# Four layers in one kernel: one arena for the head buffers, the bias of v folded away, normalisation on four engines, an order by a table of times

## What is computed

```python
h = layer_norm(x, g1, beta1)
q, k, v = h @ w_qkv + b_qkv                     # per window and head
attn = q * scale @ k.T + rel_h(q) + rel_w(q)    # bias by relative position
x = x + softmax(attn) @ v @ w_proj + b_proj
x = x + gelu(layer_norm(x, g2, beta2) @ w1 + b1) @ w2 + b2
```

## Time and profile before

| | before |
|---|---|
| runs, median (lowest, highest) | 798.07 us (797.04, 798.78) |
| profiled execution, its own time | 794.48 us |
| its span | 792.7 us |
| mean granted clock of TensorE | 0.825 |
| instructions | 13858 |

### The profile page before, as it was taken

One profiled execution on the slowest core, in us unless ns is written; L12 is line 12 of the kernel. 1 busy time (PEld: TensorE's weight loads), 2 busy tenths in 40 slices (PEclk: granted clock), 3 DMA queues, 4 the chain that ended last, 5 costly groups with the idle time before them and its releaser, 6 DMA issues.

```text
span 792.7 us, 13858 instructions
## 1 busy us (share of the span) xinstructions
PE 601.9 (76%) x5444; PEld 434.8 (55%) x5444; DVE 314.9 (40%) x846; ACT 224.7 (28%) x420; POOL 125.1 (16%) x154
## 2 busy tenths in 40 slices
PE   7737487797906988878989887387949667997677
PEld 4525365666605645645755655265726454785366
DVE  4325546526212521515242363535344652352203
ACT  2113231263400235213124433003523226222231
POOL 2120202000400231132032230010011210010001
PEclk8666756698856999979989997678986779997799
DMA  5582122130033122344022130612251302100000
GB/s 159 135 197 58 39 59 57 24 72 21 14 86 114 31 80 74 104 121 132 15 75 72 47 104 2 170 27 49 47 145 41 77 19 58 39 2 20 1 0 21
DMA packets 31913, 51.73 MB, mean 65 GB/s; under 512 B 8383, under 2 KB 12719, under 8 KB 31754
## 3 DMA queue, kind: packets, MB, share of 16 engines
q1 hardware_dynamic: 31850, 50.85, 24.8%
HBM read 10.09 MB, written 0.79 MB: 14 GB/s over the span
## 4 chain that ended last, share of the span: by engine, by line
PE 59%; DVE 16%; SPq 8%; DMA 7%; issue 5%; ACT 5%; DVEq 0%; POOL 0%; ACTq 0%
PE PS L1122 56%; DVE NM L1043 3%; DMA QA<-NR 3%; DMA COL<-in_col 2%; DVE STAT L954 2%; PE PS L1140 1%; DMA QA<-KC 1%; SPq L615 1%; PE PS L1214 1%; DVE XN L973 1%; DVE QHL L1016 1%; ACT HT L896 1%; SPq L654 1%; SPq L648 1%; DVE RSTD L965 1%
## 5 line engine op out<-in xcount | busy, mean ns | idle before, releaser
L872 ACT ACTIVATE PT<-PS 98x392 f32<-98x392 f32 (+2 forms) x192 | 96.2, 513 | 319.1 <-PE PS L1122 318.6
L1043 DVE TENSOR_REDUCE NM<-PS 98x2 fp32r<-98x392 f32 (+2 forms) x192 | 108.1, 572 | 146.4 <-PE PS L1122 145.0
L1122 PE MATMUL PS<-QA,KA 128*98 128x196 f32 (+2 forms) x528 | 124.8, 348 | 28.3 <-DMA QA<-NR 20.3
L1122 PE MATMUL PS<-KA,QA 127*98 127x196 f32 (+3 forms) x432 | 105.5, 344 | 48.5 <-issue 33.9
L1122 PEld LDWEIGHTS PS<-QA,KA 128*98 128x98 f32 (+2 forms) x528 | 89.9, 212 | 58.5 <-issue 24.7
L1122 PEld LDWEIGHTS PS<-KA,QA 127*98 127x98 f32 (+3 forms) x432 | 72.8, 217 | 69.8 <-issue 50.2
L1122 PE MATMUL PS<-XT,W 96*128 96x512 f32 x144 | 69.9, 620 | 1.3 <-ACT XT L817 1.3
L1122 PE MATMUL PS<-XT,WQKV 96*96 96x512 f32 x128 | 64.7, 635 | 1.3 <-ACT XT L817 1.3
L1214 PE MATMUL PS<-IDN,NM 120*6 120x120 f32 (+1 forms) x72 | 22.9, 318 | 54.4 <-DVE NM L1043 54.4
L1122 PE MATMUL PS<-PT,V 128*32 128x196 f32 (+2 forms) x672 | 60.6, 407 | 0.9 <-ACT PT L872 0.9
L1122 PE MATMUL PS<-W,HT 128*128 128x192 f32 x288 | 52.6, 343 | 10.9 <-ACT HT L896 10.9
(11 more groups left out here) (91 smaller groups left out, 663.2 us busy)
## 6 DMA issues: line engine op xcount, KB each, us to landing
QA<-QHL SPq DMA_DIRECT2D x72, 96.0 KB, 2.4
KA<-KHL SPq DMA_DIRECT2D x48, 141.0 KB, 2.6
QA<-REL SPq DMA_DIRECT2D x48, 128.0 KB, 2.4
QA<-QHL SPq DMA_DIRECT2D x24, 192.0 KB, 2.7
KA<-KHL SPq DMA_DIRECT2D x24, 192.0 KB, 2.7
W<-in_w SPq DMA_DIRECT2D x6, 576.0 KB, 6.5
QA<-REL SPq DMA_DIRECT2D x48, 64.0 KB, 2.2
KA<-KC SPq DMA_DIRECT2D x12, 235.0 KB
```

The costliest lines, as they stand in the source:

```text
L872: nc.scalar.activation(dst, src, ACT.Exp).then_inc(probs_done.sem, 1)
L1043: nc.vector.tensor_reduce(dst, src, AX.X, ALU.max, negate=True).then_inc(max_done.sem, 1)
L1122: return nc.tensor.matmul(dst, lhsT, rhs, start=start, stop=stop, skip_group_check=loose)
```

## The change

- **Arena.** The four head buffers become one memory ARENA of 5 slots of the wide layer; slots of both kinds are counted from its end. The wide layer's ring grows from 4 to 5. `place_of` gives a head its slot, turned so that the first heads of a new layer lie over the slots that the old one leaves first; `constants` becomes one step per slot that waits only for the last old head lying there. In padded layers two slots get their constants by one pair of DMAs, and q and k of a head go in one DMA (QKHL14 holds both), which waits for both splits.
- **v.** Its bias is no longer added. `fold` multiplies the bias by WP and adds the result to the row of WP that holds the bias of proj. v of padded layers is copied by ScalarE, that of the wide layer by VectorE. The buffers BV with padded values shrink to a constant.
- **Normalisation.** `ln` keeps the statistics on VectorE; `rs` computes the reciprocal root in sixteen operations on GpSimd; `xn` scales on ScalarE; `turn` is on TensorE as before.
- **k** of padded layers is permuted by ScalarE when it is copied out of PSUM. PT16 holds 4 heads; the clearing of PT14 is gone. gelu runs in four quarters. `norm` is two steps.
- **Spectral layer.** Both halves come at the end, in memory of their own (LATE, over the arena); s1 runs per image.
- **Loads.** The columns and relative tables of layers 1 and 2 and the second half of x are issued at the head of `weights` of phase 0.
- **Order.** `ordered` sorts the steps by a table, TIMES, with one time per step in units of heads from the phase's first scores.

```diff
-        self.ring = 6 if self.pads else 4
+        self.ring = 6 if self.pads else 5
+        self.turn = 2 if self.pads else 3
+        self.slot_room = self.tiles * (HT_ + self.keys)
+        self.const_dmas = 2 if self.pads else 3
         self.rel_row = 3 * head_dim if self.pads else head_dim
         self.mask_row = self.rel_row + (64 if self.pads else 32)
-        self.aug_dmas = 3 if self.pads else 6
+        self.aug_dmas = 2 if self.pads else 6
...
+def place_of(p, h):
+    return (HEADS * (p % 2) + h + L.turn) % L.ring
+
+def slot_start(L, s):
+
+    return L16_ROOM - (L.ring - s) * L.slot_room
+
+L16_ROOM = LAYERS[1].ring * LAYERS[1].slot_room
+
+def last_over(p, s):
+
+    L, before = PHASES[p].L, PHASES[p - 1].L
+    first, end = slot_start(L, s), slot_start(L, s) + L.slot_room
+    over = [h for h in range(HEADS - before.ring, HEADS)
+            if slot_start(before, place_of(p - 1, h)) < end
+            and slot_start(before, place_of(p - 1, h)) + before.slot_room > first]
+    return over[-1] if over else None
+
...
+TIMES = [
+    {"ln": (-7.771, 14.267,),
+     "rs": (-7.543, 14.444,),
+     "xn": (-7.314, 14.556,),
+     "turn": (-7.086, 15.208,),
...
+     "aug": (-3.886, -3.657, -2.743, -1.600, -0.229, 0.133, 1.167, 2.067, 3.167, 4.200, 5.111, 6.167,),
+     "weights": (0.833,),
+     "norm": (12.833, 13.074,),
+     "fold": (13.037,),
+     "proj": (13.733, 13.933,),
+     "up": (15.500, 15.750, 15.917, 16.278, 16.467, 16.600,),
+     "gelu": (16.792, 16.833, 16.875, 16.917,),
+     "down": (17.222, 17.467,)},
...
+     "fwd": (22.833, 24.959, 25.174, 25.390,),
+     "s1": (26.036, 26.251, 26.467, 26.682, 27.113, 27.544, 27.759, 27.974,),
+     "s2": (28.405, 28.621, 29.051, 30.559,),
+     "inv": (31.636, 31.851, 32.713, 32.928,),
+     "out": (32.282,)},
...
+     "gelu": (18.774, 18.990, 19.205, 19.421,),
+     "down": (20.067, 20.497,),
+     "fwd": (21.144, 21.359, 22.436, 22.867,),
+     "s1": (21.574, 21.790, 22.005, 22.221, 23.082, 23.728, 23.944, 24.159,),
+     "s2": (22.651, 23.297, 24.374, 24.590,),
+     "inv": (24.805, 25.021, 25.236, 25.451,),
+     "out": (23.513,)},
...
+    for p, table in enumerate(TIMES):
         L = PHASES[p].L
+        several = {"max": L.units, "scores": L.units, "pv": L.pv_steps}
+        for h in range(HEADS):
+            out += [(HEADS * p + h + k / L.units, (p, "scores", h, k)) for k in range(L.units)]
+        for step, times in table.items():
+            w = several.get(step, 1)
+            out += [(HEADS * p + t, (p, step, j // w, j % w)) for j, t in enumerate(times)]
+    return [step for _, step in sorted(out, key=lambda timed: timed[0])]
...
+    ARENA = sb(ctx, "ARENA", [128, L16_ROOM], F32R)
...
+        def lay_constants(L, s):
+
+            if L.pads:
+                two = pair(slot_start(L, s), slot_start(L, s + 1))
+                rows = 128 - L.rel_row
+                sp.dma_start(raw(two[L.rel_row:, :, HT_:]), KC14[L.rel_row:, :].unsqueeze(1).broadcast_to([rows, 2, WIN_KEYS]))\
+                    .then_inc(aug_const[s].sem, 16)
+                rows = MAX_ROW - L.mask_row
+                sp.dma_start(raw(two[L.mask_row:MAX_ROW, :, 0:HT_]),
+                             KC14[0:rows, 0:HT_].unsqueeze(1).broadcast_to([rows, 2, HT_])).then_inc(aug_const[s].sem, 16)
...
+                    at = slot_start(L, s)
+                    sp.dma_start(raw(ARENA[0:3 * hd, at:at + L.slot_room]), raw(QKHL14[mine, :, :])).then_inc(aug_in[s].sem, 16)
...
+                s = place_of(p, h)
...
+                over = last_over(p, s) if p else None
+                if p and L.pads and h % 2 == 0:
+                    over = last_over(p, s + 1)
+                if over is not None:
+                    sp.wait_ge(*scores_psum.at(p - 1, PHASES[p - 1].L.units * (over + 1) - 1))
+                if not L.pads or h % 2 == 0:
+                    lay_constants(L, s)
...
+                if p == 0:
+                    sp.dma_start(X[:, 4:8, :], xin[:, 4:8, :]).then_inc(x_in[1].sem, 16)
+                    for k in (1, 2):
+                        sp.dma_start(COL[k][:, :], io[f"col{k}"]).then_inc(col_in[k].sem, 16)
+                        sp.dma_start(RB[k][:, :, :, :], io[f"rb{k}"]).then_inc(rb_in[k].sem, 16)
+                    load_columns(0)
...
+            elif step == "rs":
+
+                pool.wait_ge(*mean_var[i].at(p, 0))
+                link(nc.gpsimd.tensor_scalar(VAR[:, :], MV[:, :, 1], L.eps, None, ALU.add))
+                link(nc.gpsimd.tensor_scalar(RSTD[:, :].bitcast(I32), VAR[:, :].bitcast(I32), -0.5, float(0x5F3759DF),
+                                             ALU.mult, ALU.add))
+                for _ in range(3):
+                    link(nc.gpsimd.tensor_tensor(SQ[:, :], RSTD[:, :], RSTD[:, :], ALU.mult))
+                    link(nc.gpsimd.tensor_tensor(SQ[:, :], SQ[:, :], VAR[:, :], ALU.mult))
+                    link(nc.gpsimd.tensor_scalar(SQ[:, :], SQ[:, :], -0.5, 1.5, ALU.mult, ALU.add))
+                    link(nc.gpsimd.tensor_tensor(RSTD[:, :], RSTD[:, :], SQ[:, :], ALU.mult))
+                link(nc.gpsimd.tensor_tensor(SQ[:, :], RSTD[:, :], MV[:, :, 0], ALU.mult))
+                nc.gpsimd.tensor_scalar(SQ[:, :], SQ[:, :], -1.0, None, ALU.mult).then_inc(rstd_done[i].sem, 1)
...
+            if step == "xn":
+                s = i
+                act.wait_ge(*rstd_done[s].at(p, 0))
+                if s == 0 and p == 1:
+                    act.wait_ge(*xt_psum[0].at(0, 1))
+                elif s == 0 and p:
+                    act.wait_ge(*xt_psum[1].at(p - 2, 1))
+                elif s == 1:
+                    act.wait_ge(*(xt_psum[0].at(p + 1, 1) if p < 5 else xt_psum[1].at(4, 1)))
+                for t in range(4):
+                    nc.scalar.activation(XN[:, t, :], X[:, ph.tile0 + t, :], ACT.Identity, scale=RSTD[:, t:t + 1],
+                                         bias=SQ[:, t:t + 1]).then_inc(xn_done[s].sem, 1)
...
+                for dst, src in in_windows(L, K[:, 0:HT_], PS[0:CK, bank[0], :]):
+                    ins = nc.scalar.activation(dst, src, ACT.Identity, bias=SKB[n][:, i:i + 1], scale=L.scale)
+                ins.then_inc(k_done.sem, 1)
...
+            elif step == "v" and L.pads:
+
+                if i == 0:
+                    act.wait_ge(*v_ones14.at(0, 1))
+                    if p and not new_layer(p):
+                        act.wait_ge(*pv_done.at(p - 1, L.groups * L.pv_steps - 1))
+                rows = HALF_IN if i < 2 * HB else EDGES
+                act.wait_ge(*v_psum.at(p, i))
+                nc.scalar.activation(V14[0:rows, i, :].rearrange("p (h d) -> p h d", h=HEADS)[:, :, 0:L.hd],
+                                     PS[0:rows, bank[0], 0:L.dim].rearrange("p (h d) -> p h d", h=HEADS), ACT.Copy)\
+                    .then_inc(v_done.sem, 1)
...
-                part = HT[:, :, i * TOK:(i + 1) * TOK]
+                part = HT[:, :, i * 128:(i + 1) * 128]
                 nc.scalar.activation(part, part, L.gelu).then_inc(gelu_done.sem, 1)
-                if i == 1:
-
-                    nc.scalar.activation(LOADED[:, :], COL[0][:, 0:2], ACT.Exp)
+                if i == 3:
...
-                link(ins)
-                link(nc.vector.tensor_scalar(VAR[:, :], MV[:, :, 1], L.eps, None, ALU.add))
-                link(nc.vector.tensor_scalar(GUESS[:, :], VAR[:, :].bitcast(I32), 1, None, ALU.logical_shift_right))
-                link(nc.vector.tensor_scalar(RSTD[:, :].bitcast(I32), GUESS[:, :], -1, 0x5F3759DF, ALU.mult, ALU.add))
-                for _ in range(3):
-                    link(nc.vector.tensor_tensor(SQ[:, :], RSTD[:, :], RSTD[:, :], ALU.mult))
-                    link(nc.vector.scalar_tensor_tensor(SQ[:, :], SQ[:, :], -0.5, VAR[:, :], ALU.mult, ALU.mult))
-                    link(nc.vector.scalar_tensor_tensor(RSTD[:, :], SQ[:, :], 1.5, RSTD[:, :], ALU.add, ALU.mult))
+                ins.then_inc(mean_var[s].sem, 1)
...
+                if i == 0:
+                    dve.wait_ge(*o_done.at(p, g - 1))
+                    dve.wait_ge(*pv_done.at(p, L.groups * L.pv_steps - 1))
+                    link(nc.vector.transpose(turned, o))
+                    link(nc.vector.reciprocal(SUMS[:, :], turned.rearrange("p (b c) -> p b c", c=32)[:, :, L.sum_row]))
+                    continue
...
+            elif step == "fold":
+
+                rows = slice(0, L.sum_row + 1)
+                dve.wait_ge(*fold_psum.at(p, 0))
+                nc.vector.tensor_tensor(WP[rows, 0, :], WP[rows, 0, :], PS[rows, bank[0], 0:C], ALU.add)\
+                    .then_inc(fold_done.sem, 1)
...
+            elif step == "fold":
+
+                pe.wait_ge(*weights_in[n].at(0, 2))
+                pe.wait_ge(*columns_in[n].at(0, 1))
+                claim(bank[0], fold_done.at(p, 0))
+                for g in range(L.groups):
+                    last = mm(PS[0:L.sum_row + 1, bank[0], 0:C], VB[n][:, g, :], WP[:, g, :], g == 0, g == L.groups - 1)
```

(7 more changed lines are left out.)

596 lines of the change are left out of this document (308 added, 288 removed).

## The result

The changed kernel takes 754.07 us (median; 750.78 to 755.51) against 797.59 for the kernel before on the same chip: a ratio of 0.9447, 95% interval 0.9413 to 0.948. Predicted were 667 us and a range of 626 to 722. The sign was right; of the 131 us of gain that were forecast, 44 came.

A forecast was written before the change was run, and what follows sets the result against it. TensorE, busy 601.9 of 792.7 us, was taken as the bound, by its stands and its clock. Idle -105, added work and stands +21, clock -44 gave 664.7, rounded to a 662 us span, 667 us as time; range 626 to 722.

The forecast's parts named there:

- The clock term: TensorE's busy time: with fewer stands the mean granted clock rises from 0.825 to about 0.89, 44 us less.
- Normalisation: Links on GpSimd and XN on ScalarE free VectorE; five stands of 25 us go to about 12, -13 us.
- the chain over four engines is the new stand: Rival: 8 us on GpSimd, ScalarE holds exponentials, each of twelve normalisations costs about 6 us; 733 us, chance 0.15.
- the last rival: Slower than before: ScalarE waits at XN for GpSimd, itself waiting, 12 us at each normalisation; 806, chance 0.03.
- The third rival: Order right on paper only: SP's issues or landings behind weights set the pace, half the idle gain lost; 747, chance 0.07.
- The 18.3 us at SKB: Phase 0 stand at VectorE's scaled bias, its columns queued behind weights; loading them earlier leaves 5 us, -13 us.
- Gelu: TensorE's waits for gelu, counted as six; quarters instead of halves let "down" start earlier, -12 us.
- The layer changes: Stands of 24.04 and 9.90 us between layers; the arena overlaps old and new layer, -22 and -7 us.
- the stands on V: Value tiles between phases, standing on VectorE; spread between scores and moved to ScalarE, part of a -13 us term.
- the row at 341.78: Stand of 7.74 us, a row of maxima behind layer 2's weights; more TensorE work ahead of it, -4 us.
- The +15 for new stands: Allowance for ScalarE's queue stopping exponentials, the fixed order and fewer fillers late in phase 5, +15 us.
- a head 3 of phase 0 that waits over 10 us: Sign to look for in phase 0: such a wait would make the sum wrong on the high side.

The follow-up runs named there:

- e12: The changed kernel with 166 dummy matmuls ahead of 20 TensorE stands and 22 instead of 14 at the start; ratio 0.9237 to the kernel before.
- e9: e2 with dummy matmuls ahead of the 22 steps where its TensorE stood over 1.4 us, and more at the start; ratio 0.9096 to the kernel before.
- e13: e5 with 184 dummy matmuls at its 25 stands; 719.39 us median, ratio 0.9081 to the kernel before.
- e2: The changed kernel with the normalisation's linked steps and XN writes put back on VectorE; ratio 0.9215 to the kernel before.
- e1: The changed kernel with phase 0's sixteen load DMAs spread between heads instead of issued in one step; ratio 0.9428 to the kernel before.
- e5: The changed kernel with both the normalisation back on VectorE and phase 0's loads spread; ratio 0.9213 to the kernel before.
- e8: The kernel before with only the two COL loads moved ahead of the weights in phase 0; ratio 0.9955 to the kernel before.
- e10: The kernel before with 290 dummy matmuls ahead of the 19 steps where TensorE stood over 3 us; ratio 1.001 to the kernel before.

## Why the prediction was wrong

**The clock term (-44, measured +2), half of the miss.** The failed step is "601.9 x (1 - 0.825/0.89)". It applies a mean over the span to the busy time. Of the 276.7 us of low level before, 93.3 passed while TensorE stood. Taking such a stand away raises the mean and speeds up nothing. To win 44 us of work at two levels a factor of two apart, 88 of the 183.4 us of own work at the low level would have to leave it; 187.3 are there after. e12, e9 and e13 have a mean clock of 0.89, 0.89 and 0.90, so the clock that I forecast could be had in this order of work. But it was had with dummies in the stands, not by stands having become shorter: twelve of over 3 us were left, and in the changed kernel each is followed by work at the low level. Of the other 7 us of the 51, 2 are half of the 3.9 us by which own work at the low level rose, and 4.5 are work that I didn't count: at the full level own work would be 607.5 - 187.3/2 = 513.9 us against 597.1 - 183.4/2 = 505.4, 8.5 more where I had 4. The row of the fold's products alone has 5.2 us, where I had 3 for it with its add.

**Normalisation (-13, measured about 0 in idle time).** The failed step is "the five stands of 25 us in sum go to about 12". They went, and the turns' stands came: 31.1 us on ScalarE's XN against 8.7 on VectorE's XN before. The link was well priced (0.28 us for the estimated 0.25, the chain 4.5 us for 4; ScalarE's XN less well, 1.86 us for four where I had 1.3), and the page on GpSimd that spoke for 0.4 us ("GPSIMD Engine Reference" of the Trainium skill, Engine selection) overstates it here, where tiles are 128x4: 0.20 us an operation against VectorE's 0.16. What I mis-sized is what lies ahead of the turn: nothing covers a chain of 1.5 + 4.5 + 1.9 us. With the clock it costs 18 us (e2) where I had 13 of gain; 31 of the missing 87 us are this one part; its 18 us are nearly all low clock, and so they are among the 46 of the clock term too. The rival "the chain over four engines is the new stand" was right that the chain becomes a stand, and put it at 66 us. It was wrong on how: TensorE stands at the turn, and not at scores behind exponentials that ScalarE holds (its waits for PT fell from 8.9 to 3.7 us), and it takes no chain of 8 us. (By its own sum its time is 734, not 733; and the 806 of the last rival is a span, as a time 811.) The third rival's 747 lies nearest to 754 of all. That is luck: it blames SP's pace, which no run shows as the limit beyond the one row below.

**The 18.3 us at SKB (-13, measured -4 in this stand).** The rival wait was named (the row of maxima behind the weights) and mis-sized: I let the transfers drain at 58 us; SP issued the row only then, and it landed 11.5 us later because the engines were full, with WQKV above all. And where a stand there was taken away on purpose (e1, e5, e8), the time answered with 0 to 4 us.

**Gelu (-12, measured -2.8).** The failed step is the count. There are three such stands, two in the earlier trace rows and a third of 3.30 us at 442.60, 10.2 us in all; I wrote of six. After, they are 2.63, 1.68, 2.44 and 1.06 us: 7.8. (With those under 1 us the group goes from 10.9 to 8.1.)

**Stands in `rel` (not in the sum, measured +13).** TensorE's idle time before `rel`'s small matmuls (Q, RB) is 5.0 us before and 18.1 after; in the change's order these steps stand back to back. The profile names no releaser ("issue"). But the trace has each transfer of instructions, and at all ten such stands of over 1 us, three before and seven after, one of 16 KB starts 2.3 to 2.8 us ahead of the stand's end. At the longest, 4.87 us at 587.29, the DMA engines are full with the spectral layer's loads (1.47 MB from 582.4 to 587.3 us). So it looks as if TensorE waits there for its own instructions; no run tests it.

**Right in size.** The layer changes (34 us to 5, predicted to 5), the stands on V (13 us, gone), the split of q (9.80, gone; I had kept 4.3), GpSimd's spectral weights (5.75, gone), the row at 341.78 (7.74, gone; I had kept 3.7) and the tail (11.7 us to 1). The +15 for new stands was near without those in `rel`: 5.21, 4.99 and 5.20 us came in phase 1.

In idle time the row (9), the normalisation (13), gelu (9) and `rel` (13) make 44 us too many; 8 came back where I had kept some (3.7 and 4.3), which leaves 36 of the 39. The signs to look for were well chosen: "a head 3 of phase 0 that waits over 10 us" came true (14.29), and ScalarE's idle time ahead of XN, to be under 3 us each, was 5.4 in the mean (59.3 us over 11).

## What to carry to other kernels

A mean clock is a mean over stands too: before it is used on busy time, lay the low windows over the work and ask which of them are idle; only low time with work in it can be won. When stands are cut from long to short, expect the idle time and not the clock, and test the clock separately with dummies that fit into the stand and write a bank that is free before the wait. A fall of low time is no gain by itself either: in e10 mean low fell by 70 us and the time not at all. A chain of small linked steps that TensorE had nothing to cover was better on the engine that starts it than spread over three, in both orders tried here (2.5% and 2.1% of the time).

## What was not expected of the hardware

Fifteen us less idle time (e8) gave 3.6 us of time; in the profile the work behind was granted a lower clock (0.66 for 0.81). Dummy matmuls in the stands made the real work 26 us faster in one kernel (607.5 to 581.7) and 5 us in another with nearly the same matmuls in another order (597.1 to 592.5). GpSimd does a linked step on 128x4 in 0.20 us, every 0.28 us, whether it has one operand or two. And each stand of TensorE of over 1 us in a `rel` step ended 2.3 to 2.8 us after a 16 KB transfer of instructions began.
